# Attention with a mixture-of-experts branch: TensorE's side work moved ahead of the weighted values in every step

## What is computed

```python
xn = _layernorm(x)
# attention: 16 heads of 8, rotary positions, softmax over 1024 keys
Q, K, V = rope(proj(W_q)), rope(proj(W_k)), proj(W_v)
scores = einsum('bhqd,bhkd->bhqk', Q, K) / sqrt(8)
attn   = softmax(scores) ; out = einsum('bhqk,bhkd->bhqd', attn, V) @ W_o.T
# experts: 8 experts of 128 -> 512 -> 128, each token goes to its best 2
w, idx = top_k(xn @ Wg, 2) ; w = softmax(w)
h   = relu(normed_e @ W1[e] + b1[e]) ; out_e = h @ W2[e] + b2[e] + xn
y   = sum over the token's two experts of w * out_e
return x + attention + y
```

## Time and profile before

| what | value |
|---|---|
| median of 3 runs | 671.93 us (671.84 to 672.0) |
| the profiled execution | 671.26 us |
| its span in the profile | 669.5 us |
| TensorE busy | 621.7 us (93%) |
| ScalarE busy | 507.3 us (76%) |
| VectorE busy | 387.9 us (58%) |
| GpSimd busy | 202.3 us (30%) |

### The profile page before, as it was taken

The page is one execution under the profiler, slowest core; times in us unless marked ns, Lnnn a source line. Parts: engine busy times, 40 slices in busy tenths (PEclk is TensorE's granted clock), DMA queues, the critical chain, the costliest instruction groups (busy, mean ns, idle before and its releaser), DMA issues.

```text
span 669.5 us, 12213 instructions
## 1 busy us (share of the span) xinstructions
PE 621.7 (93%) x4589; PEld 274.1 (41%) x4589; DVE 387.9 (58%) x1150; ACT 507.3 (76%) x551; POOL 202.3 (30%) x243
## 2 busy tenths in 40 slices
PE   3699998889999999999999999999999999999995
PEld 2224322222455555544455545544445455322222
DVE  3974669758655555587665555557766555344212
ACT  2387897888677777777777777778776777899992
POOL 0358200023763344323333343432344322100000
PEclk9889999999999999999999999999999999999997
DMA  6275702000230301200313031220031313461000
GB/s 225 55 203 155 189 1 64 0 17 21 71 88 24 87 25 48 72 17 20 83 28 86 25 87 29 52 64 17 21 87 35 73 21 76 162 198 49 16 0 34
DMA packets 25425, 43.99 MB, mean 66 GB/s; under 512 B 5472, under 2 KB 15248, under 8 KB 24848
## 3 DMA queue, kind: packets, MB, share of 16 engines
q1 hardware_dynamic: 20032, 32.15, 17.6%
q0 software_dynamic: 4608, 9.45, 5.2%
q10 hardware_dynamic: 720, 1.54, 0.6%
HBM read 17.43 MB, written 8.91 MB: 39 GB/s over the span
## 4 chain that ended last, share of the span: by engine, by line
PE 74%; ACT 11%; DVE 10%; issue 2%; DMA 1%; DVEq 1%; SPq 1%; POOL 0%; ACTq 0%
PE acc L527 28%; PE sc L494 16%; PE bank L577 12%; ACT ring L710 11%; PE bank L569 9%; PE bank L562 2%; PE bank L443 2%; PE bank L586 1%; DVE xn L1043 1%; PE bank L433 1%; PE bank L424 1%; DMA const<-shape_constants 1%; PE bank L554 1%; DVEq L1040 1%; SPq L292 1%
## 5 line engine op out<-in xcount | busy, mean ns | idle before, releaser
L710 ACT ACTIVATE ring<-sc 128x1024 f32<-128x1024 f32 x512 | 491.9, 1022 | 129.9 <-PE sc L494 129.1
L527 PE MATMUL acc<-ring,v 128*9 128x512 f32 x2048 | 270.0, 599 | 2.4 <-issue 2.4
L494 PE MATMUL sc<-qs,ks 32*128 32x512 f32 x1024 | 167.7, 500 | 19.2 <-ACT ring L710 13.0
L397 POOL DMA_INDIRECT token_out<-work,token x72 | 78.6, 1092 | 162.7 <-DVE work L1063 156.9
L387 POOL DMA_INDIRECT work<-normed,token x72 | 70.4, 978 | 172.2 <-DVE work L1049 103.0
L494 PEld LDWEIGHTS sc<-qs,ks 32*128 32x128 f32 x1024 | 65.0, 183 | 131.8 <-ACT ring L710 98.5
L577 PEld LDWEIGHTS bank<-xn,work 128*128 128x128 f32 x576 | 69.7, 191 | 65.6 <-DVE work L1056 37.7
L1056 DVE TENSOR_SCALAR work<-bank,xn 128x128 f32<-128x128 f32 x288 | 80.9, 343 | 25.3 <-PE bank L569 25.3
L577 PE MATMUL bank<-xn,work 128*128 128x128 f32 x576 | 83.1, 287 | 3.6 <-DVE work L1049 3.5
L569 PE MATMUL bank<-work,xn 128*128 128x128 f32 x576 | 77.0, 277 | 2.2 <-DVE norms L777 1.9
L569 PEld LDWEIGHTS bank<-work,xn 128*128 128x128 f32 x576 | 73.2, 197 | 4.1 <-DVE xn L1043 2.6
(11 more groups left out here) (158 smaller groups left out, 312.2 us busy)
## 6 DMA issues: line engine op xcount, KB each, us to landing
qs<-hl SPq DMA_DIRECT2D x60, 128.0 KB
ks<-hl SPq DMA_DIRECT2D x60, 128.0 KB
w_all<-L_ffn_W SPq DMA_DIRECT2D x16, 256.0 KB, 4.9
x<-L_attn_x SPq DMA_DIRECT2D x4, 512.0 KB, 7.7
normed<-xn SPq DMA_DIRECT2D x4, 512.0 KB, 5.8
xn<-token_out SPq DMA_DIRECT2D x2, 1024.0 KB, 5.9
w_all<-token_out SPq DMA_DIRECT2D x2, 1024.0 KB, 10.4
out<-x SPq DMA_DIRECT2D x8, 256.0 KB, 2.2
```

The lines of the kernel that those rows point to most:

```text
L397: pool.indirect_dma_start(out=y_d[:, :], in_=ys[done % TILE_BUFFERS], in_offset=None, out_offset=bass.IndirectOffsetOnAxis(ap=token[:, 1, ...
L494: last = nc.tensor.matmul(dst, ks[r:r + 32, kb * P:(kb + 1) * P].bitcast(F32R), qs[r:r + 32, at].bitcast(F32R), start=True, stop=not slow)
L527: last = nc.tensor.matmul(acc[qh % 2][32 * j:32 * j + VW, :], v9[:, b, kb, 4 * g + j, :], ring[:, (2 * n + j // 2) % UNITS, j % 2, :], sta ...
L710: nc.scalar.activation(ring[:, (2 * n + u) % UNITS, :, :], sc[u][:, :].rearrange("p (h c) -> p h c", h=2), ACT.Exp, scale=SCALE).then_inc( ...
```

## The change

In `attend`, which writes TensorE's list, the calls of `aside(n)` and `weigh(n)` change places. The order becomes S, A, W. Nothing else changes: the other engines' lists, the tables, the banks and every semaphore with its count are as they were.

```diff
                     if n >= 0:
                         if n % PER_BATCH == 0 and n > 0:
                             pe.wait_ge(v_ok, 4 * (n // PER_BATCH))
+                        aside(n)
                         weigh(n)
-                        aside(n)
                     if not slow and n == PER_BATCH * b + BRANCH_AT and b + 1 < B:
                         following = flag_of(b + 1)
```

## The result

The changed kernel takes 673.57 us (median of 13 runs, 672.69 to 675.82), the kernel before 671.64 in the same sessions (13 runs, 669.72 to 672.64). The ratio is 1.0040, 95% interval 1.0027 to 1.0053: 2.7 us slower (the interval is 1.8 to 3.6), where 0.98 was forecast. The profiled execution took 673.3 us; its span is 671.4 us, 1.9 above before.

A forecast was written before the change was run, and what follows sets the result against it. TensorE's own list was taken to bound the experts' part, 62% of the span; outside it TensorE and ScalarE hand score buffers to each other. Profiled: 671.26 + 0.98 + 188 × 0 = 672.24; median: 671.93 + 0.98 = 672.9 us, range 671.9 to 674.0.

The forecast's parts named there:

- The passages: TensorE's switches between S, A and W: S to A costs nothing extra, a step stays 2.50 us, 188 × 0.
- Rival 1: S to A costs as much as W to A, 0.095 us in 188 steps: 688 to 691 us; chance 0.10.
- rival 2: A's first weights load hides behind the scores, 0.05 us kept in each of 188 steps: 663.5 us; chance 0.09.
- The place: Step 30, before invert(0): W(30) no longer lies under the wait for VectorE, which grows from 1.75 to 2.73 us.
- The term of 0.98 us: From step 30 on, every S and W is 0.98 us later, and nothing gives the time back.
- The term "188 × 0": The 188 steps with side work: the new order adds nothing to any step.
- "VectorE's durations … which I took as fixed": Closing caveat: the forecast is wrong if VectorE's durations or order of waits shift with the new phase against ScalarE.
- the stacks' loads keep over 1 us of work in front of them: Flags, branches and the stacks' loads are issued ahead with over 1 us of cover, so they add nothing.
- Rival 3: W held behind a waiting A beyond invert(0): ten experts' waits grow 0.3 us each, 3 us more, 676 us; chance 0.08.

The follow-up runs named there:

- the two filled kernels: 11 matmuls nothing reads put before the wait of invert(0), in the changed kernel (672.89 us) and in the new order at step 30 only (672.80 us).
- second profile of the changed kernel: The changed kernel, unaltered, timed again in a later session against the kernel before: 674.51 us, ratio 1.0051; its profiled execution took 672.07 us.
- experiment 1: Against the kernel before, the new order in every step except 30: 672.0 us, ratio 1.0009; the new order only in step 30: 673.62 us, ratio 1.0032.
- all steps but 30: The new order in every step except step 30, which keeps W before A, against the kernel before: 672.0 us, ratio 1.0009.

## Why the prediction was right or wrong

The measured time is inside the forecast range, and slower instead of the same, to which 0.30 was given. That 673.57 us lies inside the forecast's own 671.9 to 674.0 is in part luck. The kernel before was 0.3 us quicker in these sessions than in the three runs that the sum starts from; the ratio of 1.0040 on those 671.93 would be 674.6, outside. The direction and the place were forecast, and little more than a third of the size. Point by point:

- **The passages: right.** Two rows of the kernel before and the rule read from them (0.095 us behind a matmul of 128 rows, nothing behind one of 32) gave S to A correctly, in all 188 steps. Rival 1, at 688 to 691 us, and rival 2, at 663.5, are both out: 0.44 us from S to A, and 378 ns for the first matmul. The rule was incomplete, since between like shapes there is no gap, which is worth 0.11 us in three steps.
- **The place: right.** W(30) was the cover of the wait for `mark(0)`; `tail(2)` and all of VectorE's chain behind it stayed where they were, `invert(0)` started at 105.69 us again, and W after it. The term of 0.98 us was measured as 0.97 and 1.01 in the two filled kernels.
- **The term "188 × 0" and the single 0.98: mis-sized.** What failed is the sentence that from step 30 on every S and W is 0.98 us later. It took TensorE's clock as given. At this place a wait of 2.75 us is followed by the lower clock, one of 1.75 is not. In the profiled execution S of step 33 starts at 112.59 us; before it was 110.83, and with the 0.98 it would have been 111.81. So the clock added 0.78 us, and the later steps keep it. In the second profile of the changed kernel it added 0.66, and 1.36 with the new order in step 30 alone.
- **"VectorE's durations … which I took as fixed": this is where the rest went.** The note named the wrong partner: the phase that matters is the one against the score loads, released by S, and not the one against ScalarE. The sentence that the stacks' loads keep over 1 us of work in front of them asked whether they come in time, and not what they slow down while they run. It makes a few tenths of a us in each of three steps, about 0.6 us in the time of experiment 1 and 0.8 us on average in the profiles; the first profile of the changed kernel shows only 0.12 of it.
- **Rival 3 (W held behind a waiting A in more places): not as it was put.** The waits of `layer_two` grew from seven to nine, by 0.8 us, because a read was slow and not because W lay behind A.

Together: 0.98 (order) + 0.7 (clock) + 0.6 to 0.8 (reads, less the three short passages) = 2.3 to 2.5 us, against 2.7 with an interval of 1.8 to 3.6. Not settled is why the lower clock lasts longer in some executions, as the mean clocks of 0.980 to 0.982 say; the 13 times of the changed kernel spread over 3.1 us, and no experiment separates them. Nor is it shown why VectorE's read is slow beside the load, only that it is.

## What to carry to other kernels

In a list that one engine runs in order, exchanging two pieces leaves every wait as it was if what is waited for was started by a piece of the same kind; look for the waits that are timed by something else, and there price the piece that used to lie under the wait. Then ask how long TensorE now stands still: here 1 us more of idleness also cost it its clock, and elsewhere in the same traces about 2 us were enough. And where work moves against a DMA's phase, VectorE's register reads on a tight chain can take longer than the few hundred ns that they take elsewhere.

## What the runs showed of the hardware

- After 2.73 to 2.75 us without a matmul, TensorE's granted clock was at its lower level (0.50 in a stretch of 2 us) in three profiled executions of three; at the same place it read 1.00 after 1.75 to 1.77 us, in four of four. At the end of the kernel a stop of 2.37 us was enough, and in the changed kernel's second profile one of 1.90 us wasn't, so these figures are no limit.
- The lower clock after the wait cost 0.66, 0.78 and 1.36 us in the three.
- The gap of 0.095 us follows matmuls of 128 rows at a change of shape (592 to 596 ns of a W matmul against 497 of a score matmul, both with 512 columns). It doesn't follow those of 32 rows (0.44 us from S to W and from S to A), nor a change between like shapes (0.22 us from the last `head_norms` matmul, 128 rows and 32 columns, to W with 9).
- The first 128 x 128 matmul of `layer_two` shows 378 ns in place of 275, behind W (before) and behind S (after) alike: its weights aren't loaded during either.
- VectorE's way from `rows_out` to the weights' copy at step 64, with the register read in it, took 0.48 us without the score load beside it, and 0.59, 0.75 and 1.05 with it (before, changed, all steps but 30). The read alone took 300 to 315 ns without the load, 489 to 1123 with it.
